# Route logits by 16 fp16 products in four column tiles and one folding product, with the route signs behind both rotations

## The chip, the cores and the metric

The kernel runs on one core of one Trainium2 chip. The metric is the device time of one execution in microseconds (us); the median of three runs stands for a kernel. The profile is of one execution, and its engines are named as it names them: PE is TensorE, PEld its weight loads, DVE is VectorE, ACT is ScalarE, POOL is GpSimd, SP is SyncE. A line number such as L918 is a line of the kernel before.

## The reference, cut to what matters

`x` and `ctx` are (8, 512, 1024) in float32: 4096 tokens of 1024 numbers. The layer adds a recurrent mix of `ctx` to `x` and then a gated attention over the eight batch rows of each time step:

```python
x = x + tanh(g_xattn) * wkv(time_decay, time_first, layernorm(x), ctx)
...
x = silu(x_prev * conv_w[:, 0] + x * conv_w[:, 1])       # h, from layernorm(x)
q = silu(x @ Wq); k = x @ Wk; v = x @ Wv; g = x @ Wg
q = _apply_rotary(q, cos, sin); k = _apply_rotary(k, cos, sin)
logits = jnp.einsum('bhld,hdr->bhlr', v, router_w)        # r = 2 routes, 16 heads
scores = jax.nn.softmax(logits, axis=-1)
onehot = jax.nn.one_hot(jnp.argmax(scores, axis=-1), 2)
sum_ind = jnp.cumsum(onehot, axis=2)
norm = 1.0 / jnp.maximum(sum_ind, 1.0)                    # where sum_ind > 0
q_exp = q * scores * onehot * norm; k_exp = k * onehot    # each route apart
o = (q_exp @ k_exp.T * mask) @ v
out = silu(g) * normalize(o) @ Wout
x = x + tanh(g_ffn) * out
```

With two routes only the difference of the two logits matters: its sign is the route of a head, its size the probability.

## The kernel before, in words

A tile is 16 time steps of all 8 batch rows, 128 tokens, so there are 32 tiles, called steps 0 to 31 here. Every engine runs `pipeline`, which calls its own `step` for each tile. In step i an engine does its part of tile i (`main`), of the recurrence of tile i + 1 (`nxt`), of loads for tile i + 2 (`nxt2`), and of the output of tile i - 1 (`prev`) and i - 2 (`prev2`). Nothing but the order in which `step` is written, and the semaphores, sets the order on an engine; each engine works strictly in that order.

**PE**, step i: route logits (L478, in float32), projection Q in two parts, the gate maximum's small product (L485), projection K, the running sums of the route signs (`sign_sums`, L491), projection V0, transposes of rotated q (L375), projection V1, transposes of rotated k, `same_route` (L497), projection G0, transposes of the gated output, projection G1, `scores` (L520), output projection O0 of the tile before, `xn_transposes` of tile i + 1 (L375, `ps_t<-ident,vx`), `values` (L535), O1, `values` again. A projection is 24 fp16 products of 512 columns: hi by hi (L383), hi by lo (L384) and lo by hi (L387) for eight chunks, so that two fp16 numbers stand for one float32. `same_route` waits for `s_cum`, which `route_coefficients` on DVE sets with its first instruction (L918), because it overwrites the bank that L918 reads. O0 waits for `s_gtlo`, set by L884 on DVE.

**DVE**, step i: the convolution of tile i + 1 from the transposes (`conv_products`, L1003), the low halves `h_lo` (L996), then the head sums (L841), `denominator_terms` (L813, L814, L816), the route signs (`signs`, L906 and L908), the scan (L823) and the sum of the denominator (L833), `rotate` of q (L309, L313 twice, L317), `numerator` (again L813, L814, L816, L823, L833), `route_coefficients` (L918 and four small ones), the gated output, the ratio of the recurrence, and the residual with its statistics.

**ACT**, step i: q through Silu (L634), `route_prob` (L681 and L683, a Tanh of the logits), the copy of k (L638), `seed` (L614, an Exp that needs another table), copies of v, and so on. In step 0 ACT also splits the weights of four more units (`split_unit`, L598, two halves each), the low halves of which DVE makes in `lo_unit` (L775).

**POOL**, step i: the factors of the heads, their product with the gate (L1206), the route signs spread over 512 columns (L1211), `rotate` of k (the same lines L309, L313 twice, L317), and at the end the scales of the norms.

The names: `fa` holds h in float32 while the logits are made, `h_hi` and `h_lo` are its fp16 halves, `w_route` the router folded into the V weights (128 x 8 chunks x 16 heads), `big` is one buffer with many views (the weights, q, k, v, gates, `route`), `small` holds narrow columns, `ps_t`, `ps_g`, `ps_s`, `ps_o` are PSUM banks. Ahead of `pipeline` DVE prepares scales, tables, the folded router (`route_chunk`, L782) and the centred V weights (`centre`, L792, L794, L798).

## Time and profile before

| | us |
|---|---|
| median of three runs | 1753.68 |
| the three runs | 1753.19, 1753.68, 1754.88 |
| the profiled execution, its own time | 1754.45 |
| its span, from the first to the last instruction | 1752.7 |
| PE busy | 1624.3 (93%) |
| DVE busy | 1465.3 (84%) |
| ACT busy | 741.6 (42%) |
| POOL busy | 612.2 (35%) |

The profiled execution took 0.77 us more than the median, and 1.75 us lie around its span. The page's slices show PE busy at 9 tenths from the sixth of 40 slices to the 39th and at the full clock there; in the first five slices DVE is busier than PE.

In a row of the timeline the columns are the start and the length in us, then engine, line, operation, output and input by name, shapes, the count of merged instructions, and in brackets the idle time of the engine before the row with what ended it. Matmuls overlap, so the distance between two starts is what a matmul costs, not its length.

### The profile page before, as it was taken

The numbers are of one execution on the slowest core, as the hardware profiler recorded it, in microseconds if no ns is written. First come the engines' busy times: TensorE is split into PE (matmuls) and PEld (weight loads), VectorE is DVE, ScalarE is ACT, GpSimd is POOL, SyncE is SP. The second block draws the span as 40 slices with busy tenths as digits, with TensorE's granted clock in tenths as the row PEclk, the third lists the DMA queues.
The fourth block names the chain that finished last, engine by engine and source line by source line (L and its number), as shares of the span: only waits on it lengthen the run. The fifth ranks groups of instructions, "written<-read, shape, count | busy, mean of one in ns | idle before, by whom it ended". The sixth has DMA issues, their size and how long they took to land.

```text
span 1752.7 us, 37624 instructions
## 1 busy us (share of the span) xinstructions
PE 1624.3 (93%) x15799; PEld 866.7 (49%) x15799; DVE 1465.3 (84%) x2004; ACT 741.6 (42%) x933; POOL 612.2 (35%) x716
## 2 busy tenths in 40 slices
PE   0445999999999999999999999999999999999996
PEld 0123555555555555555555555555555555555552
DVE  7898988888889888888898888888888888889832
ACT  4835344344443443444434434444344444443420
POOL 1421433443223434432234344322343444223321
PEclk9867999999999999999999999999999999999998
DMA  9500011111100111111111111110001111100000
GB/s 269 191 13 25 5 33 37 37 38 38 28 25 30 29 37 37 37 38 29 27 30 28 37 37 38 37 35 24 30 25 37 38 37 38 37 25 26 14 13 25
DMA packets 23416, 70.77 MB, mean 40 GB/s; under 512 B 2256, under 2 KB 2512, under 8 KB 23248
## 3 DMA queue, kind: packets, MB, share of 16 engines
q1 hardware_dynamic: 23248, 68.37, 13.6%
q8 instruction: 125, 2.05, 0.5%
q14 instruction: 43, 0.35, 0.1%
HBM read 51.59 MB, written 16.78 MB: 39 GB/s over the span
## 4 chain that ended last, share of the span: by engine, by line
PE 88%; DVE 8%; issue 2%; ACT 1%; POOL 1%; DMA 0%; SPq 0%; POOLq 0%; DVEq 0%; ACTq 0%
PE ps_g L383 25%; PE ps_g L384 24%; PE ps_g L387 24%; PE ps_o L535 4%; PE ps_t L478 3%; PE ps_t L375 3%; PE ps_o L375 2%; DVE big L775 2%; PE ps_t L520 1%; PE ps_s L520 1%; DVE seg L823 1%; DVE big L792 0%; PE ps_s L497 0%; DVE seg L814 0%; DMA small<-in_g_ffn 0%
## 5 line engine op out<-in xcount | busy, mean ns | idle before, releaser
L383 PE MATMUL ps_g<-big,h_hi 128*128 128x512 f16 x1536 | 585.5, 381 | 3.2 <-DVE h_lo L996 3.2
L384 PE MATMUL ps_g<-big,h_hi 128*128 128x512 f16 x1536 | 585.4, 381 | 0.0
L387 PE MATMUL ps_g<-big,h_lo 128*128 128x512 f16 x1536 | 584.9, 381 | 0.0
L387 PEld LDWEIGHTS ps_g<-big,h_lo 128*128 128x128 f16 x1536 | 150.7, 98 | 183.8 <-issue 4.2
L1149 POOL TENSOR_TENSOR small<-small 128x1 f32<-128x1 f32 x64 | 14.2, 221 | 648.8 <-DVE small L808 648.6
L383 PEld LDWEIGHTS ps_g<-big,h_hi 128*128 128x128 f16 x1536 | 158.7, 103 | 165.0 <-issue 7.3
L384 PEld LDWEIGHTS ps_g<-big,h_hi 128*128 128x128 f16 x1536 | 150.7, 98 | 165.3 <-issue 3.4
L383 PE MATMUL ps_g<-big 128*128 128x512 f16 x512 | 195.3, 382 | 0.7 <-DVE big L884 0.7
L384 PE MATMUL ps_g<-big 128*128 128x512 f16 x512 | 194.8, 380 | 0.0
L387 PE MATMUL ps_g<-big 128*128 128x512 f16 x512 | 194.7, 380 | 0.0
L1168 POOL TENSOR_TENSOR vx<-vx,ek 128x1024 f32<-128x1024 f32 x32 | 75.3, 2353 | 337.0 <-ACT ek L607 326.1
L823 DVE TENSOR_TENSOR_SCAN seg<-decay,seg 128x1088 f32<-128x1088 f32 x64 | 155.0, 2421 | 1.1
L713 ACT ACTIVATE big<-ps_g,small 128x512 f32<-128x512 f32 x64 | 44.0, 687 | 207.3 <-PE ps_g L387 207.3
L694 ACT ACTIVATE fa<-fa 128x1024 f32<-128x1024 f32 x32 | 33.8, 1058 | 229.7 <-DVE fa L990 229.7
L841 DVE TENSOR_REDUCE small<-big 128x16 f32<-128x1024 f32 x32 | 39.0, 1220 | 71.9 <-ACT big L630 71.9
L1193 POOL TENSOR_TENSOR small<-small 128x16 f32<-128x16 f32 x32 | 93.3, 2914 | 2.5
L804 DVE BATCH_NORM_STATS2 small<-x_ring 128x6 f32<-128x512 f32 x128 | 82.0, 683 | 7.3 <-DMA x_ring<-in_x 6.1
L1206 POOL TENSOR_TENSOR big<-big,small 128x1024 f32<-128x1024 f32 x32 | 86.6, 2706 | 2.5
L1003 DVE TENSOR_TENSOR fa<-ps_t,small 128x512 f32<-128x512 f32 x64 | 43.9, 686 | 49.7 <-PE ps_t L375 49.7
L313 DVE TENSOR_TENSOR big<-big,sin 128x256 f32<-128x256 f32 x64 | 84.2, 1354 | 0.0
L996 DVE SCALAR_TENSOR_TENSOR h_lo<-fa,small,h_hi 128x512 f16<-128x512 f32 x64 | 47.5, 784 | 39.3 <-ACT h_hi L700 39.3
L387 PEld LDWEIGHTS ps_g<-big 128*128 128x128 f16 x512 | 50.2, 98 | 60.9 <-issue 0.8
(158 smaller groups left out, 2902.5 us busy)
## 6 DMA issues: line engine op xcount, KB each, us to landing
x_ring<-in_x SPq DMA_DIRECT2D x32, 512.0 KB
vx<-in_ctx SPq DMA_DIRECT2D x32, 512.0 KB
out<-x_ring SPq DMA_DIRECT2D x32, 512.0 KB
big<-in_wv SPq DMA_DIRECT2D x2, 2048.0 KB, 21.1
big<-in_wg SPq DMA_DIRECT2D x2, 2048.0 KB, 20.7
big<-in_wout SPq DMA_DIRECT2D x2, 2048.0 KB, 20.1
big<-in_wq SPq DMA_DIRECT2D x1, 2048.0 KB, 14.5
big<-in_wk SPq DMA_DIRECT2D x1, 2048.0 KB, 20.1
```

The costliest lines, as they stand in the source:

```text
L313: E.tensor_tensor(t4[:, :, s, :], s4[:, :, 1 - s, :], sin2[:, s * half:(s + 1) * half].rearrange("p (o d) -> p o d", o=1) .to_broadcast([P ...
L375: last = nc.tensor.transpose(order(dst[:, n * P:(n + 1) * P]), src[:, n * P:(n + 1) * P], ident[:, :])
L383: nc.tensor.matmul(dst[:, :], hi, hi_of(u)[:, kc * HALF:(kc + 1) * HALF], start=(kc == 0), stop=False)
L384: nc.tensor.matmul(dst[:, :], hi, lo_of(u)[:, kc * HALF:(kc + 1) * HALF], start=False, stop=False)
L387: last = nc.tensor.matmul(dst[:, :], lo, hi_of(u)[:, kc * HALF:(kc + 1) * HALF], start=False, stop=(kc == KC - 1))
L478: last = nc.tensor.matmul(ps_t[1][:, 0:H], fa[:, kc * P:(kc + 1) * P], w_route[:, kc * H:(kc + 1) * H], start=(kc == 0), stop=(kc == KC - 1))
L535: last = nc.tensor.matmul(ps_o[g][rows, (h - 8 * g) * DV:(h - 8 * g + 1) * DV], probs[rows, h * BLK:(h + 1) * BLK], v[rows, h * DV:(h + 1) ...
L804: last = V.bn_stats(st[:, 6 * g:6 * g + 6], src[:, g * HALF:(g + 1) * HALF])
L823: V.tensor_tensor_scan(seg[:, :], decay[:, :], seg[:, :], 0.0, ALU.mult, ALU.add).then_inc(scanned, 1)
L1168: G.tensor_tensor(vx[:, :], vx[:, :], ek[:, :], ALU.mult).then_inc(s_ev, 1)
L1193: G.tensor_tensor(fac, ftmp, nhalf, ALU.pow).then_inc(s_fp, 1)
L1206: G.tensor_tensor(by_head(sg, DV), by_head(sg, DV), per_head(fac, 0, H, DV), ALU.mult)\
```

## The change

Four edits that belong together:

- **The logits on PE.** The eight float32 products of `fa` with `w_route` go. In their place stand 16 fp16 products, `h_hi` and `h_lo` as moving operands of 128 columns, against `w_route_hl`, 32 columns a chunk (16 of a high half, 16 of a low half). Chunk kc writes 32 rows of the bank, (kc mod 4) x 32 onwards, which are four column tiles of the array. ACT copies the 128 x 128 result to `logits_t` (`copy_logits`), and one float32 product with `r_sum` folds the eight groups of 16 rows and scales them. The 16 products stand behind Q, the folding product behind K.
- **The split of the router's weights.** `split_route_weights` on DVE, ahead of `pipeline`, with a maximum over 1024 columns earlier on.
- **The signs.** On DVE they stand behind the rotation of q instead of ahead of the scan; on PE `sign_sums` stands behind V0 instead of ahead of it; on ACT `route_prob` stands behind the copy of k and in front of `seed` (there it waits for the first instruction of the signs).
- **POOL** rotates k in front of spreading the signs.

```diff
@@ PE, step
                 if main:
-                    if not opening(i):
-                        route_logits(i)
                     unit_ready(i, UQ)
...
                     gate_max_turn(p)
                 if main:
+                    if not opening(i):
+                        route_products(i)
                     unit_ready(i, UK)
                     bank_free(i, 1, prev2)
                     project(ps_g[1], h_hi, h_lo, UK, s_kp)
                     if opening(i):
                         for r in range(5, 9):
                             bound_row(r)
-                        pe.wait_ge(s_wroute, 8)
-                        route_logits(i)
-                    sign_sums(i)
+                        pe.wait_ge(s_rw, 8)
+                        route_products(i)
+                    route_logits(i)
                     unit_ready(i, UV)
                     after(pe, s_q, i + 1)
                     project(ps_g[0], h_hi, h_lo, UV, s_vp)
+                    sign_sums(i)
@@ PE
+            def route_products(i):
+
+                after(pe, s_hlo, 2 * (i + 1))
+                for a in (h_hi, h_lo):
+                    for kc in range(KC):
+                        rows = slice(kc % 4 * 2 * H, (kc % 4 + 1) * 2 * H)
+                        last = nc.tensor.matmul(ps_t[1][rows, 0:P], w_route_hl[:, kc * 2 * H:(kc + 1) * 2 * H],
+                                                a[:, kc * P:(kc + 1) * P], start=(a is h_hi and kc < 4),
+                                                stop=(a is h_lo and kc >= 4))
+                last.then_inc(s_dlp, 1)
+
             def route_logits(i):
 
-                after(pe, s_h, i + 1)
-                for kc in range(KC):
-                    last = nc.tensor.matmul(ps_t[1][:, 0:H], fa[:, kc * P:(kc + 1) * P], w_route[:, kc * H:(kc + 1) * H],
-                                            start=(kc == 0), stop=(kc == KC - 1))
-                last.then_inc(s_dl, 1)
+                after(pe, s_dlc, i + 1)
+                nc.tensor.matmul(ps_t[1][:, P:P + H], logits_t, r_sum, start=True, stop=True).then_inc(s_dl, 1)
@@ ACT, step
                     if not opening(i):
-                        route_prob(i)
+                        copy_logits(i)
                     act.wait_ge(s_kp, i + 1)
                     A(k_sb, ps_g[1][:, :], ACT.Copy, scale=inv[:, UK:UK + 1]).then_inc(s_k, 1)
                     if opening(i):
-                        route_prob(i)
+                        copy_logits(i)
+                    route_prob(i)
                 if nxt:
                     seed(n)
@@ ACT
+            def copy_logits(i):
+                act.wait_ge(s_dlp, i + 1)
+                after(act, s_dl, i)
+                A(logits_t, ps_t[1][:, 0:P], ACT.Copy).then_inc(s_dlc, 1)
@@ DVE, ahead of the pipeline
+            def split_route_weights():
+
+                V.tensor_reduce(r_sum, ident[:, :].rearrange("p (j h) -> p h j", h=H), AX_X, ALU.add).then_inc(s_rw, 1)
...
+                V.tensor_scalar(r_bound, r_max, mx[:, UV:UV + 1], mx[:, UV + 1:UV + 2], ALU.mult, ALU.max).then_inc(s_rw, 1)
...
+                V.tensor_scalar(r_bound, r_bound, TINY, None, ALU.max).then_inc(s_rw, 1)
...
+                V.reciprocal(r_scale, r_bound).then_inc(s_rw, 1)
...
+                V.tensor_scalar(r_scale, r_scale, W_TOP, None, ALU.mult).then_inc(s_rw, 1)
+                V.tensor_scalar(r_inv, r_bound, mx[:, U:U + 1], LN_BOUND / (W_TOP * H_TOP), ALU.mult, ALU.mult)\
+                 .then_inc(s_rw, 1)
...
+                V.tensor_scalar(r_sum, r_sum, r_inv, None, ALU.mult).then_inc(s_rws, 1)
+                V.tensor_scalar(hl[:, :, 0, :], rows, r_scale, None, ALU.mult).then_inc(s_rws, 1)
+                dve.wait_ge(s_rws, 2)
+                V.scalar_tensor_tensor(hl[:, :, 1, :], rows, r_scale, hl[:, :, 0, :], ALU.mult, ALU.subtract)\
+                 .then_inc(s_rw, 1)
...
             tokens_by_time()
+            dve.wait_ge(s_base, 1)
+            V.tensor_reduce(r_max, x_ring[:, 2, :], AX_X, ALU.max, apply_absolute_value=True).then_inc(s_rw, 1)
...
                 route_chunk(m)
+            split_route_weights()
             centre(UV + 1)
@@ DVE, step
                     denominator_terms(n)
-                if main:
-                    signs(i)
-                if nxt:
                     denominator_scan(n)
...
                     rotate(dve, V, i, 0, q_sb, rot_q, s_r1q, s_rq)
+                    signs(i)
                     if opening(i):
                         lo_unit(4)
@@ POOL, step
                 if main:
+                    pool.wait_ge(s_k, i + 1)
+                    after(pool, s_op, 2 * i)
+                    rotate(pool, G, i, 1, k_sb, rot_k, s_r1k, s_rk)
                     pool.wait_ge(s_sgn, i + 1)
                     after(pool, s_rt, i)
                     G.tensor_tensor(by_head(route, BLK), per_head(sgn, 0, H, BLK),
                                     fold.rearrange("p (o l) -> p o l", o=1).to_broadcast([P, H, BLK]), ALU.mult)\
                      .then_inc(s_route, 1)
-                    pool.wait_ge(s_k, i + 1)
-                    after(pool, s_op, 2 * i)
-                    rotate(pool, G, i, 1, k_sb, rot_k, s_r1k, s_rk)
```

What stands in a row on DVE in the middle of a step, from the last denominator term to the first instruction of the numerator, first before and then after the change (L906 and L908 are the signs, L948 and L950 in the changed kernel):

```order
L816 TENSOR_TENSOR fa<-seg,small 128x1024
L906 TENSOR_SCALAR small<-ps_t 128x16
L908 TENSOR_SCALAR small<-small 128x16
L823 SCALAR_TENSOR_TENSOR seg<-decay,seg 128x1088
L825 COPY carry_b<-seg 128x64
L833 TENSOR_TENSOR fa<-fa,seg 128x1024
L913 TENSOR_TENSOR small<-small,ps_s 128x2
L309 TENSOR_TENSOR big<-big,cos 128x512
L313 TENSOR_TENSOR big<-big,sin 128x16x16 x2
L317 TENSOR_TENSOR big<-big 128x512
L813 COPY seg<-carry_a 128x64
```

```order
L860 TENSOR_TENSOR fa<-seg,small 128x1024
L867 SCALAR_TENSOR_TENSOR seg<-decay,seg 128x1088
L869 COPY carry_b<-seg 128x64
L877 TENSOR_TENSOR fa<-fa,seg 128x1024
L955 TENSOR_TENSOR small<-small,ps_s 128x2
L314 TENSOR_TENSOR big<-big,cos 128x512
L318 TENSOR_TENSOR big<-big,sin 128x16x16 x2
L322 TENSOR_TENSOR big<-big 128x512
L948 TENSOR_SCALAR small<-ps_t 128x16
L950 TENSOR_SCALAR small<-small 128x16
L857 COPY seg<-carry_a 128x64
```

The same eleven instructions stand there; the two signs moved from the second place to the last but one, behind the four of the rotation.

On POOL, from the gate's product on (L1206, L1250 after), before and after; L1211 and L1258 spread the signs:

```order
L1206 TENSOR_TENSOR big<-big,small 128x1024
L1211 TENSOR_TENSOR big<-small,big 128x512
L309 TENSOR_TENSOR big<-big,cos 128x512
L313 TENSOR_TENSOR big<-big,sin 128x16x16 x2
L317 TENSOR_TENSOR big<-big 128x512
```

```order
L1250 TENSOR_TENSOR big<-big,small 128x1024
L314 TENSOR_TENSOR big<-big,cos 128x512
L318 TENSOR_TENSOR big<-big,sin 128x16x16 x2
L322 TENSOR_TENSOR big<-big 128x512
L1258 TENSOR_TENSOR big<-small,big 128x512
```

The spreading of the signs moved from in front of the four instructions of the rotation to behind them.

On ACT in step 0, from the Silu of q to the next weights' high halves (L598 before, L612 after), before and after:

```order
L634 ACTIVATE big<-ps_g,small 128x512
L638 ACTIVATE big<-ps_g,small 128x512
L681 ACTIVATE small<-ps_t 128x16
L683 ACTIVATE small<-small 128x16
L614 ACT_TABLE_LOAD
L614 ACTIVATE ek<-fa,small 128x1024
L598 ACTIVATE big<-big,small 128x2048 x2
```

```order
L648 ACTIVATE big<-ps_g,small 128x512
L652 ACTIVATE big<-ps_g,small 128x512
L696 ACTIVATE big<-ps_t 128x128
L701 ACTIVATE small<-ps_t 128x16
L703 ACTIVATE small<-small 128x16
L628 ACT_TABLE_LOAD
L628 ACTIVATE ek<-fa,small 128x1024
L612 ACTIVATE big<-big,small 128x2048 x2
```

Here ACT keeps its order but for the added copy (L696); what moved is the sign on DVE that L701 waits for.

## Rows read from the trace of the kernel before

**Rows 1.** Busy us of PE, PEld, DVE, ACT, POOL, then clock, DMA share, GB/s, 214:1664

```profile
214.00:1664.00 1450.00, 1449.99 (x14308) 774.63 (x14306) 1251.86 (x1712) 618.74 (x812) 533.93 (x636) 1.00 0.12 33
```

**Rows 2.** Timeline of PE in one middle step: logits, sign sums, same_route, next transposes

```profile
872.96 1.96 PE L478 MATMUL ps_t<-big,fa 128*128 128x16 f32 x16
874.77 0.38 PE L383 MATMUL ps_g<-big,h_hi 128*128 128x512 f16 x1
...
885.26 0.29 PE L491 MATMUL ps_s<-small,causal_m 128*128 128x16 f32 x2
885.40 0.38 PE L383 MATMUL ps_g<-big,h_hi 128*128 128x512 f16 x1
...
896.63 0.38 PE L497 MATMUL ps_s<-big 128*128 128x512 bf16 x1
```

**Rows 3.** Timeline of DVE in the same step, from the convolution to route_coefficients

```profile
865.39 0.69 DVE L1003 TENSOR_TENSOR fa<-ps_t,small 128x512 f32<-128x512 f32 x1 [1.62 <-PE ps_t L375]
...
875.36 1.22 DVE L841 TENSOR_REDUCE small<-big 128x16 f32<-128x1024 f32 x1 [2.33 <-ACT big L630]
...
878.03 1.23 DVE L816 TENSOR_TENSOR fa<-seg,small 128x1024 f32<-128x1024 f32 x1
879.18 0.17 DVE L906 TENSOR_SCALAR small<-ps_t 128x16 f32<-128x16 f32 x1
...
879.46 2.42 DVE L823 TENSOR_TENSOR_SCAN seg<-decay,seg 128x1088 f32<-128x1088 f32 x1
...
883.28 2.32 DVE L309 TENSOR_TENSOR big<-big,cos 128x512 f32<-128x512 f32 x1
885.52 2.67 DVE L313 TENSOR_TENSOR big<-big,sin 128x256 f32<-128x256 f32 x2
888.23 1.10 DVE L317 TENSOR_TENSOR big<-big 128x512 f32<-128x512 f32 x1
889.26 0.74 DVE L813 COPY seg<-carry_a 128x64 f32<-128x64 f32 x1
...
896.14 0.17 DVE L918 TENSOR_TENSOR small<-ps_s,small 128x16 f32<-128x16 f32 x1
```

**Rows 4.** Timeline of step 1: its convolution, same_route on PE, the next convolution

```profile
166.34 0.69 DVE L1003 TENSOR_TENSOR fa<-ps_t,small 128x512 f32<-128x512 f32 x1
...
197.39 0.38 PE L497 MATMUL ps_s<-big 128*128 128x512 bf16 x1 [0.72 <-DVE small L918]
...
216.11 0.69 DVE L1003 TENSOR_TENSOR fa<-ps_t,small 128x512 f32<-128x512 f32 x1 [1.47 <-PE ps_t L375]
```

**Rows 5.** Timeline of POOL and ACT in the middle step, beside the rotation of q

```profile
885.01 1.50 POOL L1211 TENSOR_TENSOR big<-small,big 128x512 bf16<-128x512 f32 x1
885.47 0.69 ACT L638 ACTIVATE big<-ps_g,small 128x512 f32<-128x512 f32 x1 [4.31 <-PE ps_g L387]
...
886.47 1.44 POOL L309 TENSOR_TENSOR big<-big,cos 128x512 f32<-128x512 f32 x1
...
890.00 1.28 POOL L317 TENSOR_TENSOR big<-big 128x512 f32<-128x512 f32 x1
```

**Rows 6.** Timeline of the setup: one short DVE instruction beside POOL, and without it

```profile
75.99 2.37 POOL L1176 TENSOR_TENSOR big<-big,x_ring 128x1024 f32<-128x1024 f32 x1
...
77.73 0.69 DVE L794 TENSOR_SCALAR big<-big 128x64 f32<-128x64 f32 x1
...
94.35 0.20 DVE L794 TENSOR_SCALAR big<-big 128x64 f32<-128x64 f32 x1
```

**Rows 7.** Timeline of step 0: ACT's table, seed and weight halves; DVE's low half

```profile
117.42 1.28 ACT L614 ACT_TABLE_LOAD   x1
...
122.66 1.15 ACT L614 ACTIVATE ek<-fa,small 128x1024 f32<-128x1024 int32 x1 [3.95 <-DVE fa L833]
123.71 3.88 ACT L598 ACTIVATE big<-big,small 128x2048 f16<-128x2048 f32 x2
...
126.68 4.80 DVE L775 SCALAR_TENSOR_TENSOR big<-big,small 128x2048 f16<-128x2048 f32 x2
```

More of the change, by code:

```diff
@@ L127, in flamingo_layer @@
         w_route = turn[:, P:2 * P]
+        w_route_hl = turn[:, 2 * P:3 * P].bitcast(F16)
+        logits_t = turn[:, 3 * P:4 * P]
         q_sb = work[:, 4 * C:4 * C + HALF]
@@ L148, in flamingo_layer @@
         cnt_c = sb("cnt_c", [P, 1])
-        small = sb("small", [P, 373])
+        small = sb("small", [P, 378])
         at = [0]
@@ L185, in flamingo_layer @@
         usc = col(2)
+        r_max, r_bound, r_scale, r_inv = col(1), col(1), col(1), col(1)
+        r_sum = col(H)
         seed_b, minus_one, half_c = col(1), col(1), col(1)
@@ L680, in route_prob @@
                 after(act, s_cf, i)
-                A(pr, ps_t[1][:, 0:H], ACT.Abs).then_inc(s_th, 1)
+                A(pr, ps_t[1][:, P:P + H], ACT.Abs).then_inc(s_th, 1)
                 act.wait_ge(s_th, 2 * i + 1)
@@ L784, in route_chunk @@
                  .then_inc(s_wroute, 1)
+            def split_route_weights():
+                V.tensor_reduce(r_sum, ident[:, :].rearrange("p (j h) -> p h j", h=H), AX_X, ALU.add).then_inc(s_rw, 1)
+                dve.wait_ge(s_rw, 2)
+                dve.wait_ge(s_wsc, UV + 2)
+                V.tensor_scalar(r_bound, r_max, mx[:, UV:UV + 1], mx[:, UV + 1:UV + 2], ALU.mult, ALU.max).then_inc(s_rw, 1)
+                dve.wait_ge(s_rw, 3)
+                V.tensor_scalar(r_bound, r_bound, TINY, None, ALU.max).then_inc(s_rw, 1)
+                dve.wait_ge(s_rw, 4)
+                V.reciprocal(r_scale, r_bound).then_inc(s_rw, 1)
+                dve.wait_ge(s_rw, 5)
+                V.tensor_scalar(r_scale, r_scale, W_TOP, None, ALU.mult).then_inc(s_rw, 1)
+                V.tensor_scalar(r_inv, r_bound, mx[:, U:U + 1], LN_BOUND / (W_TOP * H_TOP), ALU.mult, ALU.mult)\
+                 .then_inc(s_rw, 1)
+                dve.wait_ge(s_rw, 7)
+                dve.wait_ge(s_wroute, 8)
+                hl = w_route_hl.rearrange("p (k s h) -> p k s h", s=2, h=H)
+                rows = w_route.rearrange("p (k h) -> p k h", h=H)
+                V.tensor_scalar(r_sum, r_sum, r_inv, None, ALU.mult).then_inc(s_rws, 1)
[3 more added lines that the diff above has]
+                 .then_inc(s_rw, 1)
             def centre(u):
@@ L905, in signs @@
                 after(dve, s_cump, i)
-                V.tensor_scalar(sgn, ps_t[1][:, 0:H], 0.0, 2.0, ALU.is_ge, ALU.mult).then_inc(s_sgp, 1)
+                V.tensor_scalar(sgn, ps_t[1][:, P:P + H], 0.0, 2.0, ALU.is_ge, ALU.mult).then_inc(s_sgp, 1)
                 dve.wait_ge(s_sgp, i + 1)
@@ L940, in denominator_terms @@
                 after(dve, s_pre, n)
-                after(dve, s_dl, n)
                 recurrence_terms(n, ek[:, :], carry_b, s_sva, s_ekt, fa[:, :], s_fda)
```

3 lines of the change are left out of this document (2 added, 1 removed).

## The prediction

> **What bounds the kernel now.** I read the busy time by stretch first. From 214 to 1664 us PE is busy all 1450 us at the full clock, and DVE 1251.86 us of it [rows 1]. So PE is the bound of the steady part, and a microsecond less on PE in each step seems to be worth 31 us. The timeline of one step tells how far that holds. A cycle is the time from one convolution to the next: 216.11 to 865.39 is 13 cycles, 49.94 us each [rows 3, 4]. DVE's idle times in it are 1.62 us before the convolution, where it waits for PE's transposes, and 2.33 us before the head sums, where it waits for ACT [rows 3]. From there to L918 one instruction follows the other. And PE waits for L918 before same_route: L918 ends at 896.31, same_route starts at 896.63 [rows 2, 3]. Step 1 shows how much of these 0.32 us is slack. There PE was early, idle for 0.72 us until L918, and same_route started 0.31 us after L918's start, against 0.49 us in the middle step. Slack is 0.18 us. The cycle of step 1 took 49.77 us [rows 4]. That is the floor which the loop through DVE sets, whatever PE does: transposes of the next tile, convolution, ACT, DVE's chain to L918, same_route, and PE's work from same_route to the next transposes, which the change leaves alone. PE's work that does get shorter lies beside DVE's chain.
>
> **PE, part by part.** Removed: the eight float32 products, 872.96 to 874.77, 1.81 us a step [rows 2]. Added: the folding product. A float32 product of 16 columns costs 885.26 to 885.40, 0.14 us [rows 2]. Added: 16 fp16 products of 128 columns in four column tiles. No row has that form. Upper bound: a product record of L478 costs 1.81 / 16 = 0.113 us with its weight load behind nothing, so 16 cost 1.81 us. Lower bound: a projection's product of 512 columns goes on every 0.216 us, so 128 columns are 0.054 us, and four rounds of four tiles at once are 0.22 us. I take 0.5 us, near the lower end, since the work of a full round is at most a quarter of a projection's and two changes of the array's form have to be paid; it lies in PE's cover anyway. PE's own cycle would then be 49.94 - 1.81 + 0.14 + 0.5 = 48.77 us, 1.0 us under the floor of 49.77. Nearly all of the gain turns into a wait, and the question is what the change does to the floor.
>
> **DVE's chain.** The signs leave their place ahead of the scan. L816 ends at 879.26 and the scan started at 879.46; it can start some 0.04 us after L816, so 0.16 us are gained there [rows 3]. Next is the rotation. Its four instructions are long because DVE and POOL take turns: L309 takes 2.32 us, the second and third 2.67 us together, L317 1.10 us, while POOL runs without a gap [rows 3, 5]. Before, three POOL instructions take their turn between the end of L309 and the end of L317: L1211, L309 and the first L313. After, POOL has the rotation of k first, so they are L309 and both L313. For that k must be there by the end of DVE's L309 at 885.44. k's copy ended at 885.47 + 0.69 = 886.16 [rows 5]; K's end moves forward by the logits and back by the 16 products, 1.81 - 0.5 = 1.31 us, so k is there at 884.85. The turn of L1211 lasted from DVE's end of L309 at 885.60 to 886.51, 0.91 us; the turn of the second L313 lasted from the end of L317 at 889.33 to 890.00 less 0.08 of the copy, 0.59 us. The exchange gains 0.32 us, and L317 ends at 889.33 - 0.16 - 0.32 = 888.85. POOL's L317 follows, which takes 1.14 to 1.28 us [rows 5], to 890.0 to 890.13.
>
> Now the signs stand here. The first reads PSUM and can run beside it. The second goes from SBUF to SBUF like L794, which took 0.69 us beside a POOL instruction and 0.20 us without one [rows 6]. So I let it wait for POOL's L317. It ends at about 890.15, the copy L813 (0.22 us free of POOL, starting 0.09 before that end) at 890.25 instead of 890.00. The chain to L918 is 0.25 us longer and the floor 50.02 us.
>
> The Trainium skill (SBUF — State Buffer, Who interferes with whom) says that a tensor_scalar or copy from SBUF to SBUF can take a form that uses both ports, and that it then waits until GpSimd's instruction has ended. The trace agrees, 0.69 against 0.20 us; by that rule the second sign waits too.
>
> Projection V0 began at 885.40 and takes 24 x 0.216 = 5.18 us; now it ends 1.31 us earlier, at 889.3. There PE meets the sign sums, and the sign is ready at 890.15, a wait of about 0.9 us; V1 and the transposes then end by 896.6, as L918's result allows same_route at 896.7. The spreading of the signs on POOL starts at 890.2 and needs 0.91 us; the next DVE instruction with two inputs in SBUF starts at 891.4, so it doesn't meet it. ACT waits for the first sign until 889.0 and then has Tanh, table and seed done by 892; the ratio needs them at 898. That wait costs nothing in a steady step.
>
> Thirty cycles lie between the convolution of step 1 and that of tile 31 (166.34 to 1664.4, 1498.0 us: one of 49.77 and 29 of 49.94). After: 30 x 50.02 = 1500.6, **+2.6 us**. The last step has no recurrence on DVE, PE sets it, and it gains 1.81 - 0.64 = **-1.2 us**.
>
> **Setup and step 0.** Until about 196 us the chain of work that ended last runs through DVE, so DVE's additions count in full. One maximum over 1024 columns, 1.2 us (as L841 [rows 3]); one reduction, 0.3; six short instructions of 0.20 (as L794 alone [rows 6]), 1.2; two of 128 columns, 0.3 each: **+3.3 us**, with no idle time of DVE behind them that they fill. In step 0 the second weight split waits on ACT. ACT's table load stood at 117.42 and was done long before the seed at 122.66; the weight halves ran from 123.71 and DVE's L775 took them without a wait at 126.68 [rows 7]. After, signs come behind the rotation. POOL rotates k earlier there, which by the turns above ends DVE's rotation some 1.7 us earlier, so the sign is at ACT by 125.2 on the same scale; then 0.45 for Abs and Tanh, 1.28 table, 1.15 seed, 1.95 for the first half: L775 can start at 130.05 instead of 126.68, **+3.4 us** (+5 if the rotation ends no earlier, 0 if DVE's later waits in this step would have come anyway; none stands in its timeline).
>
> **The sum.** 3.3 + 3.4 + 2.6 - 1.2 = +8.1 us on the profiled execution's 1754.45, 1762.6 us; less its 0.77 us over the median, 1761.8.
>
> **Rivals.**
> (a) The second sign does not wait for POOL (for it: it has 16 columns, L794 had 64; against: rows 6). The copy L813 waits for it instead, the chain is 0.07 us longer, the floor 49.84: 30 x 49.84 - 1498.0 = -2.8. Sum 3.3 + 3.4 - 2.8 - 1.2 = +2.7, 1756.4 us. Within 0.2%, not slower.
> (b) DVE's chain opens up: if k came after DVE has done its four instructions, they would not share turns with POOL, the chain would be over 2 us shorter and PE's own 48.77 us would hold: 30 x 48.77 - 1498.0 = -34.9, sum -29.4, 1724 us, faster. It decides at a k ready after 887, against 884.85 by my sum; partly late values lie between.
> (c) The column tiles don't run side by side, so the change doesn't do on PE what it says: 16 products cost 1.81 + 0.1 us. PE's cycle is 50.18, over the floor. 30 x 50.18 - 1498.0 = +7.4; last step +0.2; sum 14.3, 1768 us. It decides from 1.7 us on. The Trainium skill (TensorE: Matmul & The Clock Gate, Part 3, The mechanism) says that a weight load overlaps a matmul in flight only when the row group differs; column tiles share all rows, so that rule speaks for (c). The rows show only that loads do hide in the full-array form.
> (d) POOL's spreading of the signs catches the next two-input instruction on DVE and pushes it by 0.9 us: floor 50.8, +25 us more, 1784 us. The margin is 0.2 us.
>
> **Chances.** Forecast 0.48, (a) 0.27, (b) 0.08, (c) 0.10, (d) 0.07. The range 1755 to 1769 takes in (a), the forecast with +3.4 to +5 in step 0, and (c). Measurement of this kernel tells 0.2%, 3.5 us, from no change. Slower by more: nearly all of the forecast, a fifth of (a), (c) and (d), 0.69. Same: 0.23. Faster: 0.08.
>
> **What the profile after would show.** In a middle step PE idle for about 1.0 us in all, before the sign sums (released by the second sign) and before same_route (by the changed L918), DVE's distance from convolution to L918's start 31.0 us against 30.75, cycles of 50.0 us; the 16 products within 0.3 to 0.7 us; in step 0 DVE idle for 4 to 5 us before its low half, released by ACT. Wrong would be: PE busy without a gap and cycles under 49.5 us (b), or over 50.1 with no gap (c).

## The result, and the profile after

The changed kernel takes 1758.33 us (median of 12 runs, 1757.57 to 1759.41) against 1754.53 us for the kernel before on the same chips: ratio 1.0023, with a 95% interval of 1.0014 to 1.0032. It is slower by 3.8 us. The profiled spans are 1756.2 and 1752.7 us.

Busy time first: the page's line of busy time and share of the span, then the stretch of [rows 1], with the same columns.

```profile
PE 1598.1 (91%) x15863; PEld 821.9 (47%) x15863; DVE 1468.7 (84%) x2014; ACT 746.7 (43%) x965; POOL 602.2 (34%) x716
```

```profile
214.00:1664.00 1450.00, 1428.26 (x14486) 735.20 (x14483) 1256.76 (x1716) 624.03 (x842) 527.76 (x640) 1.00 0.12 33
```

PE was busy all 1450 us before [rows 1]; now it is idle for 21.7 of them, and nothing is won: in the steady part the cycle, the distance from one convolution to the next, has a median of 49.91 us against 49.93. PE's waits from 215 to 1670 us say where the idle time is (engine, tile and line waited for; total us, times, longest):

```profile
PE ps_s L505 <- DVE small L950: 20.6, 29, 1.0
```

L505 are the sign sums and L950 is the second sign. PE's timeline of a middle step (start, us, line, form; in brackets the idle time and who ended it), as [rows 2]:

```profile
883.55 0.28 PE L499 MATMUL ps_s<-small,big 128*128 128x1 f32 x2
883.76 0.30 PE L486 MATMUL ps_t<-h_hi,big 128*32 128x128 f16 x8
883.88 0.29 PE L486 MATMUL ps_t<-h_lo,big 128*32 128x128 f16 x8
884.10 0.39 PE L388 MATMUL ps_g<-big,h_hi 128*128 128x512 f16 x1
...
895.45 0.40 PE L505 MATMUL ps_s<-small,causal_m 128*128 128x16 f32 x2 [0.68 <-DVE small L950]
...
901.97 0.38 PE L511 MATMUL ps_s<-big 128*128 128x512 bf16 x1
```

The 16 products (L486) take 0.34 us, from 883.76 to 884.10, where the eight float32 ones took 1.81. DVE in the same step, as [rows 3]:

```profile
870.79 0.69 DVE L1044 TENSOR_TENSOR fa<-ps_t,small 128x512 f32<-128x512 f32 x1 [1.48 <-PE ps_t L380]
...
880.76 1.22 DVE L885 TENSOR_REDUCE small<-big 128x16 f32<-128x1024 f32 x1 [2.33 <-ACT big L644]
...
888.51 2.32 DVE L314 TENSOR_TENSOR big<-big,cos 128x512 f32<-128x512 f32 x1
890.75 2.36 DVE L318 TENSOR_TENSOR big<-big,sin 128x256 f32<-128x256 f32 x2
893.14 1.10 DVE L322 TENSOR_TENSOR big<-big 128x512 f32<-128x512 f32 x1
894.16 0.16 DVE L948 TENSOR_SCALAR small<-ps_t 128x16 f32<-128x16 f32 x1
894.36 1.03 DVE L950 TENSOR_SCALAR small<-small 128x16 f32<-128x16 f32 x1
895.31 0.21 DVE L857 COPY seg<-carry_a 128x64 f32<-128x64 f32 x1
...
896.67 1.22 DVE L860 TENSOR_TENSOR fb<-seg,small 128x1024 f32<-128x1024 f32 x1
...
901.65 0.17 DVE L960 TENSOR_TENSOR small<-ps_s,small 128x16 f32<-128x16 f32 x1
...
920.70 0.69 DVE L1044 TENSOR_TENSOR fa<-ps_t,small 128x512 f32<-128x512 f32 x1 [1.47 <-PE ps_t L380]
```

And ACT's copy of k and POOL beside it, as [rows 5]:

```profile
889.49 0.69 ACT L652 ACTIVATE big<-ps_g,small 128x512 f32<-128x512 f32 x1 [4.89 <-PE ps_g L392]
890.25 1.70 POOL L314 TENSOR_TENSOR big<-big,cos 128x512 f32<-128x512 f32 x1
891.92 1.78 POOL L318 TENSOR_TENSOR big<-big,sin 128x256 f32<-128x256 f32 x2
893.77 1.59 POOL L322 TENSOR_TENSOR big<-big 128x512 f32<-128x512 f32 x1
895.47 1.05 POOL L1258 TENSOR_TENSOR big<-small,big 128x512 bf16<-128x512 f32 x1
```

The second sign (L950) has 16 columns and takes 1.03 us: it ends at 895.39, right behind POOL's L322 (895.36). The carry copy behind it is ready at 24.73 us after the convolution, 24.61 before. From the convolution to the start of route_coefficients (L960) it is 30.86 us, against 30.75 before [rows 3].

Step 0 is the other place. ACT's wait for the first sign, and DVE's wait for ACT's weight half, which was not there in [rows 7]:

```profile
127.34 0.18 ACT L701 ACTIVATE small<-ps_t 128x16 f32<-128x16 f32 x1 [10.77 <-DVE small L948]
...
130.13 3.88 ACT L612 ACTIVATE big<-big,small 128x2048 f16<-128x2048 f32 x2
132.15 2.35 DVE L795 SCALAR_TENSOR_TENSOR big<-big,small 128x2048 f16<-128x2048 f32 x1 [4.64 <-ACT big L612]
```

| stretch | before, us | after, us | difference | forecast |
|---|---|---|---|---|
| to the last low half of the setup (L775, L795) | 109.54 | 112.05 | +2.51 | +3.3 |
| to the convolution in step 1 | 166.34 | 171.81 | +5.47 in all, so step 0 +2.96 | +6.7, step 0 +3.4 |
| 30 cycles, to the convolution of tile 31 | 1498.09 | 1498.24 | +0.15 | +2.6 |
| last step, to its same_route | 31.24 | 30.04 | -1.20 | -1.2 |
| from there to the end of DVE's last instruction | 50.68 | 49.78 | -0.90 | 0 |

The last output's DMA follows, 6.3 us in both. Together the differences are +3.5 us, that of the profiled spans.

### The profile page after: what moved, and what is told of

Its sections match the earlier page's. It is cut to its first block, busy times and chain, and to the rows that moved or that the text cites. A ratio compares the mean times of both kernels' runs of the same rounds, so it can differ in the third digit from the quotient of the medians.

```text
span 1756.2 us, 37826 instructions
## 1 busy us (share of the span) xinstructions
PE 1598.1 (91%) x15863; PEld 821.9 (47%) x15863; DVE 1468.7 (84%) x2014; ACT 746.7 (43%) x965; POOL 602.2 (34%) x716
## 3 DMA queue, kind: packets, MB, share of 16 engines
q8 instruction: 125, 2.05, 0.5%
## 4 chain that ended last, share of the span: by engine, by line
PE 46%; DVE 35%; ACT 10%; issue 8%; POOL 1%; DMA 0%; DVEq 0%; SPq 0%; ACTq 0%; POOLq 0%
PE ps_g L388 13%; PE ps_g L392 12%; PE ps_g L389 12%; DVE seg L867 5%; DVE big L318 4%; DVE big L314 4%; DVE fa L860 2%; PE ps_t L380 2%; DVE seg L858 2%; DVE seg L1047 2%; ACT L621 2%; DVE fa L877 2%; DVE fa L1031 2%; ACT fa L714 2%; ACT ek L621 2%
## 5 line engine op out<-in xcount | busy, mean ns | idle before, releaser
L388 PEld LDWEIGHTS ps_g<-big,h_hi 128*128 128x128 f16 x1536 | 153.5, 100 | 174.1 <-issue 11.2
L389 PEld LDWEIGHTS ps_g<-big,h_hi 128*128 128x128 f16 x1536 | 150.9, 98 | 165.3 <-issue 3.6
L733 ACT ACTIVATE big<-ps_g,small 128x512 f32<-128x512 f32 x64 | 43.4, 678 | 106.0 <-PE ps_g L392 106.0
L1250 POOL TENSOR_TENSOR big<-big,small 128x1024 f32<-128x1024 f32 x32 | 86.7, 2708 | 2.5
L652 ACT ACTIVATE big<-ps_g,small 128x512 f32<-128x512 f32 x32 | 22.0, 687 | 151.4 <-PE ps_g L392 151.4
L634 ACT ACTIVATE ek<-fa,small 128x1024 f32<-128x1024 f32 x32 | 36.8, 1149 | 106.7 <-DVE fb L1002 106.7
```

The source lines that it names most:

```text
L388: nc.tensor.matmul(dst[:, :], hi, hi_of(u)[:, kc * HALF:(kc + 1) * HALF], start=(kc == 0), stop=False)
L389: nc.tensor.matmul(dst[:, :], hi, lo_of(u)[:, kc * HALF:(kc + 1) * HALF], start=False, stop=False)
L1250: G.tensor_tensor(by_head(sg, DV), by_head(sg, DV), per_head(fac, 0, H, DV), ALU.mult)\
```

## The experiments

In the order in which they ran. A cycle is the median of the distances between convolutions. Differences from "the changed kernel" are from its 1758.33 us; ratios are to the kernel before, run beside the variant.

**DVE's denominator ahead of the head sums**, in the changed kernel and in the one before (there with `signs` left behind it):

```diff
+                if nxt:
+                    denominator_terms(n)
                 if prev:
                     dve.wait_ge(s_sq, 2 * (p + 1))
                     V.tensor_reduce(ossq, ...)
                 if nxt:
-                    denominator_terms(n)
                     denominator_scan(n)
```

> The changed kernel with DVE's copy, transpose and product of the denominator (for the next tile) put ahead of the head sums, into the place where DVE waits 2.33 us for ACT's squares. Theory (the loop through DVE sets the cycle, PE has room): DVE waits only until ACT's second exponential has ended at 879.76 and the scan starts at about 883.55 instead of 884.68, so the cycle falls from 49.91 by up to 1.1 us to 48.8, still over PE's own 48.6: 30 x 1.1 = 33 us less, 1725 us. Rival 1 (PE's own time sets the cycle, the 16 products cost what they replace): 1758 us, no change, and PE without a gap. Rival 2 (the head sums come 1.5 us later, POOL's head factors, gate product and rotation of k follow, and PE waits for the rotated k): the cycle falls by 0.3 to 0.6 us only, 1740 to 1750 us, with PE's wait at the transposes of k.

> The same exchange on DVE, made in the kernel before (float32 logits on PE, signs ahead of the scan). Theory (two limits within 0.2 us of each other, PE's own 49.9 and DVE's loop 49.77): only DVE's loop gets shorter, PE's own 49.9 us stays, so the cycle moves by at most 0.05 us: 1752 to 1755 us, no change. Rival (PE was never a limit, only DVE's loop): the cycle falls by as much as in the changed kernel, 15 to 33 us in all, 1721 to 1740 us.

Measured: 1873.2 us (ratio 1.068) and 1907.49 us (1.087), cycles of 54.2 and 55.0 us. Neither expectation held. DVE's gap was filled, and the loss came through POOL, far beyond what rival 2 had put on it. The timeline of DVE and POOL in the changed kernel's variant, and PE's waits (215 to 1660 us):

```profile
885.14 2.41 DVE L867 TENSOR_TENSOR_SCAN seg<-decay,seg 128x1088 f32<-128x1088 f32 x1
885.30 2.26 POOL L1230 TENSOR_TENSOR small<-small 128x16 f32<-128x16 f32 x1 [2.29 <-DVE small L887]
...
896.51 1.93 POOL L1251 TENSOR_TENSOR big<-big,small 128x1024 f32<-128x1024 f32 x1
```

```profile
PE ps_t L380 <- POOL big L322: 59.0, 27, 2.5
PE ps_s L511 <- POOL big L1259: 33.3, 27, 1.3
```

A head factor of 16 columns (L1230) takes 2.26 us beside the scan, against 0.22 where it stood beside DVE's transpose. One by one they meet the scan and the products; the gate product starts 24.92 us after the convolution (896.51 - 871.59) instead of 16.73, and POOL's rotation and the signs' spreading behind it make PE wait. So the 2.33 us gap of DVE isn't free: work put into it delays the head sums, and POOL gets its operands from them. For the two limits this pair settles nothing, since a third one, POOL, was made the bound in both.

**Step 0: the weight half first.**

```diff
-                    route_prob(i)
+                    else:
+                        route_prob(i)
 ...
                     if opening(i):
                         split_unit(4)
+                        route_prob(i)
```

> The changed kernel with one edit in step 0 alone: ACT takes the seed and the high half of the fifth weight unit first, and the Abs and Tanh of the route logits behind them, so that the weight half no longer waits for the first sign, which now stands behind DVE's rotation. Theory (the late sign costs 2.96 us through ACT in step 0): 2.0 to 3.0 us less than the changed kernel, about 1755.5 us; DVE's wait for ACT in front of the low half falls from 4.64 to under 2 us. Rival (another wait of step 0, for PE or for the next low half, comes as late anyway): within 0.5 us of the changed kernel, 1758 us.

Measured: 1754.74 us (1753.48 to 1756.68), 3.6 under the changed kernel and more than the 2 to 3 expected; cycles as in it, 49.91; the convolution in step 1 at 168.37 instead of 171.81. DVE's wait fell from 4.64 to 0.82 us. That takes back 3.44 us where step 0 had lost 2.96, so ACT's wait for the sign was the whole of step 0's term.

**The 16 products four times.**

```diff
-                for a in (h_hi, h_lo):
+                for a in (h_hi, h_lo, h_hi, h_lo, h_hi, h_lo, h_hi, h_lo):
```

> The changed kernel with the 16 products of a step issued four times over (64 products; the result is the same, since each round of sums starts anew). It prices the products and PE's room in the cycle. Theory (16 products cost 0.25 to 0.35 us, since four column tiles run side by side, and PE has 1.0 us of room a cycle, most of it in front of the sign sums): 48 more products are 0.75 to 1.05 us, they fill the room, and the cycle grows by 0 to 0.1 us: 1758 to 1762 us. Rival (column tiles run one after the other, 0.05 to 0.1 us a product): 48 more cost 2.6 to 5.4 us, 1.6 to 4.4 of them over the room: 1806 to 1890 us.

Measured: 1753.79 us, 4.5 us *less* than the changed kernel, cycle 49.73. Neither had that. The price of the products was right: a step's eight L486 groups follow each other at 0.11 us, 0.0143 us a product.

```profile
882.31 0.30 PE L486 MATMUL ps_t<-h_hi,big 128*32 128x128 f16 x8
...
883.11 0.29 PE L486 MATMUL ps_t<-h_lo,big 128*32 128x128 f16 x8
883.32 0.39 PE L388 MATMUL ps_g<-big,h_hi 128*128 128x512 f16 x1
```

PE's work grew by 0.67 us and its waits at the sign sums fell from 20.6 to 0.8 us. The gain is on DVE (this kernel's convolution is at 869.35):

```profile
888.72 0.69 ACT L652 ACTIVATE big<-ps_g,small 128x512 f32<-128x512 f32 x1 [5.00 <-PE ps_g L392]
889.29 1.82 DVE L318 TENSOR_TENSOR big<-big,sin 128x256 f32<-128x256 f32 x2
889.48 1.35 POOL L314 TENSOR_TENSOR big<-big,cos 128x512 f32<-128x512 f32 x1 [0.66 <-ACT big L652]
...
892.37 0.50 DVE L950 TENSOR_SCALAR small<-small 128x16 f32<-128x16 f32 x1
...
894.15 2.12 DVE L860 TENSOR_TENSOR fb<-seg,small 128x1024 f32<-128x1024 f32 x1
```

k is there at 889.41, 20.06 us after the convolution, instead of 19.39. DVE's first rotation instruction ends at 20.02, so its second is already running when POOL begins, and the two L318 take 1.82 instead of 2.36 us. The numerator's product (L860) then meets POOL and takes 2.12 instead of 1.22 us, which gives most of it back; 0.18 us a cycle stay.

**No rotation of k on POOL**, in both kernels (it is left out; k goes to PE as it is):

```diff
-                    rotate(pool, G, i, 1, k_sb, rot_k, s_r1k, s_rk)
...
-                    transposes(ps_t[1], rot_k, s_ktp, as_is)
+                    transposes(ps_t[1], k_sb, s_ktp, as_is)
```

> The changed kernel without POOL's rotation of k (its four instructions are left out, PE transposes k as ACT wrote it, so the scores are not the reference's). Theory (the cycle of the changed kernel is set by DVE's chain, and that by the turns which DVE and POOL take, while PE has about 1.0 us of room): DVE's rotation behind its first instruction is no longer shared, DVE's loop falls by over 2 us to about 47.2, and PE's own time shows, 49.91 - 1.0 = 48.9 us a cycle: 1728 us (1722 to 1735). Rival (PE has no such room, its saving is not there): under 0.3 us a cycle, 1750 us or more.

> The same left out of the kernel before (the scores are not the reference's). Theory (PE's own time is at the limit there, with the float32 logits in it): the cycle stays within 0.1 us of 49.93, 1751 to 1755 us, though DVE's loop falls by about 2 us. Rival (only DVE's loop sets the cycle in both kernels): it falls as in the changed kernel without the rotation, to 1722 to 1735 us.

Measured: 1721.65 us (ratio 0.981) and 1751.42 us (0.998). Cycles 48.73 and 49.93. The view of busy time, 300 to 1600 us, of the changed kernel, of it without the rotation, and of the kernel before without it:

```profile
300.00:1600.00 1300.00, 1280.40 (x12878) 658.69 (x12876) 1126.71 (x1537) 558.85 (x754) 472.80 (x572) 1.00 0.12 33
```

```profile
300.00:1600.00 1300.00, 1298.64 (x13260) 678.53 (x13285) 1081.04 (x1571) 571.97 (x774) 350.80 (x482) 1.00 0.12 34
```

```profile
300.00:1600.00 1300.00, 1298.63 (x12807) 695.17 (x12831) 1074.32 (x1536) 553.58 (x731) 357.39 (x468) 1.00 0.12 33
```

With DVE's chain shortened (the coefficients start at 28.08 us after the convolution in the changed kernel without the rotation) PE is busy throughout in both, and the cycle is PE's own: 49.93 us before the change, 48.73 after. The change does save 1.20 us of PE a step, and in the real kernel all of it is hidden behind DVE's chain. The same removal is worth 36.7 us after the change and 3.7 us before it, and of these 3.7 nothing is in the cycle.

**POOL's old order** in the changed kernel (spreading the signs ahead of the rotation of k):

> The changed kernel with POOL's order of before: the spreading of the signs first, the rotation of k behind it. Since the signs now stand behind DVE's rotation, POOL starts the rotation of k only when DVE's is done. Theory (the exchange on POOL is needed once the signs are moved): DVE's rotation is over about 2 us sooner, but POOL rotates k from about 893.7 on, in turns with the numerator's products and behind its scan, and is done about 900, where PE wants k at 896.6: cycle 52 to 53.5 us, 1820 to 1870 us, PE waiting at the transposes of k for POOL. Rival (POOL keeps up, the order on POOL is of no account): 1755 to 1761 us.

Measured: 1764.56 us (ratio 1.0053), cycle 50.18. The direction is the theory's, the size is a tenth of it. DVE's rotation did end 2.0 us sooner (21.43 us after the convolution, 23.45 in the changed kernel), and POOL's work met the numerator (POOL's timeline, convolution at 873.23, and PE's waits):

```profile
897.27 4.51 POOL L318 TENSOR_TENSOR big<-big,sin 128x256 f32<-128x256 f32 x2
901.87 2.25 POOL L322 TENSOR_TENSOR big<-big 128x512 f32<-128x512 f32 x1
```

```profile
PE ps_t L380 <- POOL big L322: 34.9, 28, 1.6
```

POOL is done at 904.12, 30.89 us after the convolution. PE's transposes of k start at 904.26 after a wait of 1.25 us, so PE wanted it at 29.78. The size in the expectation was a slip: its 900 us was on the clock of the trace after (29.2 us after the convolution there) and its 896.6 on that of the trace before (31.2 us after it). Set against one convolution, POOL was to be done before PE wants it, and the wait comes from its being done 1.7 us later than estimated.

**POOL's rotation waits for DVE's first rotation instruction.**

```diff
                     after(pool, s_op, 2 * i)
+                    pool.wait_ge(s_r1q, 3 * i + 1)
                     rotate(pool, G, i, 1, k_sb, rot_k, s_r1k, s_rk)
```

> The changed kernel with one wait more: POOL's rotation of k also waits for DVE's first rotation instruction of the same step. In the run with 64 products k came 0.7 us later, just behind that instruction, and the cycle was 49.73 us; here k is as early as in the changed kernel and PE has no work more. Theory (the late k itself gave that: DVE's second instruction gets in ahead of POOL's first, and DVE is done 0.5 us sooner): cycle 49.7 to 49.8, 1752 to 1755 us, and PE idle again for about 0.8 us before the sign sums. Rival (the work on PE gave it, by no waits of PE at the sign sums): cycle 49.91, 1758 us.

Measured: 1751.32 us (1750.54 to 1753.03), ratio 0.9979 with an interval of 0.9969 to 0.9988; cycle 49.73. It is the late start of POOL's rotation, not PE's extra work, that gave the gain: k is as early as in the changed kernel (19.39) and PE again waits, about 1.0 us a step. It does so for route_coefficients (L960), not in front of the sign sums as expected. One added wait beats both kernels.

Nine of the 30 cycles are shorter, mostly 49.57 us. In both kinds POOL's spreading of the signs (L1258) and DVE's product (L860) start within 0.01 us of each other, 24.82 us after the convolution. In 21 cycles POOL is first: L860 takes about 2.12 us and the scan behind it 2.42. In nine DVE is: 1.22 and 3.15, and the coefficients start at 30.54 instead of 30.71.

**The signs in one instruction.**

```diff
-                V.tensor_scalar(sgn, ps_t[1][:, P:P + H], 0.0, 2.0, ALU.is_ge, ALU.mult)
-                V.tensor_scalar(sgn, sgn, -1.0, None, ALU.add)
+                V.tensor_scalar(sgn, ps_t[1][:, P:P + H], 0.0, 0.5, ALU.is_ge, ALU.subtract)
```

> The changed kernel with the signs taken in one instruction that reads PSUM and gives +0.5 and -0.5 (the count of signs is then multiplied by 4, exactly), so there is no second sign that goes from SBUF to SBUF. Theory (what costs is the turn of POOL's last rotation instruction, which any copy or sign from SBUF to SBUF waits for): the carry copy behind it waits for the same POOL instruction, so DVE's chain is shorter by 0 to 0.1 us; cycle 49.8 to 49.92, 1755 to 1758.5 us; PE's wait at the sign sums falls to about 0.2 us, and PE waits later. Rival (the second instruction and its wait are themselves the cost, as the forecast had it with 0.25 us and more): cycle 49.65 or less, under 1751 us.

Measured: 1757.21 us, cycle 49.84. As the theory had it: the carry copy now waits for the same POOL instruction, 1.20 us long, and the second sign costs 0.07 us a cycle. PE's wait in front of the sign sums is gone, and PE waits in front of same_route instead, for the first of the route coefficients (L958 here; same_route's own record is missing in this trace, so the wait is shown at the product behind it). The waits from 215 to 1640 us:

```profile
PE ps_g L388 <- DVE small L958: 31.8, 28, 1.2
```

So the sign sums were where PE waited, and not what set the cycle.

```profile
893.55 1.60 POOL L322 TENSOR_TENSOR big<-big 128x512 f32<-128x512 f32 x1
893.94 0.16 DVE L948 TENSOR_SCALAR small<-ps_t 128x16 f32<-128x16 f32 x1
894.03 1.20 DVE L857 COPY seg<-carry_a 128x64 f32<-128x64 f32 x1
```

**All 16 products in one column tile.**

```diff
-                        rows = slice(kc % 4 * 2 * H, (kc % 4 + 1) * 2 * H)
+                        rows = slice(0, 2 * H)
```

> The changed kernel with all 16 products in one column tile of 32 rows (one sum over the eight chunks and both halves, the folding product over 32 rows; the result is the same up to rounding). Theory (the four tiles run side by side, 0.0143 us a product in the run of 64): one tile costs a projection's rate, 128 of 512 columns of 0.216 us, 0.054 us a product, 16 in 0.87 us, 0.6 more than with four tiles; k then comes 0.6 us later, just about with the end of DVE's first rotation instruction, and the cycle is between 49.73 and 49.91: 1753 to 1758 us. Rival (the tiles don't matter, consecutive products overlap anyhow): 16 in 0.25 to 0.35 us and 1758 us.

Measured: 1755.52 us, cycle 49.74.

```profile
883.04 0.62 PE L486 MATMUL ps_t<-h_hi,big 128*32 128x128 f16 x8
883.50 0.61 PE L486 MATMUL ps_t<-h_lo,big 128*32 128x128 f16 x8
884.04 0.39 PE L388 MATMUL ps_g<-big,h_hi 128*128 128x512 f16 x1
```

The products take 1.00 us instead of 0.34, a little over the 0.87 expected: eight of them 0.46 us in one tile, where eight in the row of 64 over four tiles took 0.11. The four column tiles do run side by side. k comes at 20.05, with the end of DVE's first instruction, so the kernel with the dearer products is 2.8 us faster than the changed one.

**Both repairs together**, then the wait for the third rotation instruction (`3 * i + 3`) in place of the first.

> The changed kernel with two of the edits above together: in step 0 ACT takes the weight half ahead of Abs and Tanh, and POOL's rotation of k waits for DVE's first rotation instruction. Theory (the two act in different places, step 0 and the cycle, and add up): 7.0 + 3.6 us under the changed kernel's 1758.3, 1747.7 us (1746.5 to 1749). Rival (they overlap, or the wait on POOL was already what helped in step 0): 1750 to 1751.5 us.

> As the run before, but POOL's rotation of k waits for DVE's third rotation instruction. Theory (every POOL instruction that gets its turn inside DVE's rotation costs DVE a turn): DVE's second and third take 0.4 us each, its last still meets POOL's first, and the rotation ends about 0.4 us sooner than with the wait for the first; POOL's last rotation instruction ends no sooner and pushes the numerator's product as before, so of the 0.4 us between none and all reaches the cycle: 49.35 to 49.75, 1736 to 1749 us. Rival (the k rotation comes too late for PE or pushes the numerator's product further): cycle over 49.8, 1751 us or more, with PE waiting for the rotated k or for the route coefficients.

Measured: 1748.21 us (0.9964, 0.9949 to 0.9978) and 1742.22 us (0.9927, 0.9912 to 0.9942). The two add up, 10.1 us against 3.6 + 7.0. The wait for the third gives a cycle of 49.51. Its step (convolution at 861.27):

```profile
881.23 0.75 DVE L318 TENSOR_TENSOR big<-big,sin 128x256 f32<-128x256 f32 x2
882.01 0.69 DVE L322 TENSOR_TENSOR big<-big 128x512 f32<-128x512 f32 x1
882.14 1.69 POOL L314 TENSOR_TENSOR big<-big,cos 128x512 f32<-128x512 f32 x1 [1.39 <-DVE big L318]
...
885.15 1.22 DVE L862 TENSOR_TENSOR fb<-seg,small 128x1024 f32<-128x1024 f32 x1
885.32 2.17 POOL L322 TENSOR_TENSOR big<-big 128x512 f32<-128x512 f32 x1
886.40 3.37 DVE L869 TENSOR_TENSOR_SCAN seg<-decay,seg 128x1088 f32<-128x1088 f32 x1
```

DVE's rotation meets no POOL instruction any more and ends 21.43 us after the convolution instead of 23.45. The expectation had its last instruction meet POOL's first; it did not. POOL's turns come later, one of them ahead of the scan (3.37 instead of 2.42 us), and route_coefficients start at 30.47 instead of 30.86. It is the fastest version here that still computes the layer, 16.1 us under the changed kernel.

| kernel | k there | DVE's rotation ends | carry copy ends | coefficients start | cycle |
|---|---|---|---|---|---|
| before | 20.77 | 23.94 | 24.61 | 30.75 | 49.93 (PE) |
| after | 19.39 | 23.45 | 24.73 | 30.86 | 49.91 |
| products x4 | 20.06 | 22.90 | 23.64 | 30.68 | 49.73 |
| one tile | 20.05 | 22.91 | 23.66 | 30.70 | 49.74 |
| k after the first | 19.39 | 22.92 | 23.67 | 30.71 | 49.73 |
| k after the third | 19.39 | 21.43 | 22.72 | 30.47 | 49.51 |
| one sign | 19.39 | 23.45 | 24.67 | 30.81 | 49.84 |
| POOL's old order | 19.39 | 21.43 | 21.95 | 29.69 | 50.18 (POOL) |
| after, k not rotated | 19.39 | 21.42 | 21.95 | 28.08 | 48.73 (PE) |

Times in us after the convolution of a middle step. The last column is the median cycle.

The table shows which wait sets the cycle. In the six kernels where it names neither PE nor POOL, the cycle is 19.02 to 19.05 us longer than the start of the coefficients, whatever PE does before it; in step 1 before it is 19.03 (197.39 - 0.31 - 166.34 = 30.74, of 49.77). Where PE or POOL is the bound it is 19.18 or more.

## Why the prediction was right, and where its sizes were off

The forecast was slower, because PE's saving turns into a wait while setup and step 0 get longer. That is what happened, and the runs without k's rotation show it: PE's own cycle is 48.73 us, worked out as 48.77. The sum was +8.1 us, and it is +3.8 (+3.5 in the profiled spans). That is in the range, but nearer to the +2.7 of rival (a) than to the forecast, though (a)'s mechanism was not at work, and only just outside the 3.5 us that the prediction counted as no change. The steady part, to which most of the working went, gave next to nothing; slower came from setup and step 0, +5.47 us together. That the direction stood with a floor priced at twice its size is in part luck. Four terms carry the difference: the floor 2.4 us of it, setup 0.8, step 0 0.4 and the stretch behind the last step 0.9.

- **The floor.** This is the term that was mis-sized most: +0.25 us was worked out, and +0.11 (30.86 - 30.75) to +0.14 (49.91 - 49.77 in step 1 before) came. That is a cycle of 49.91 instead of 50.02, and 30 cycles gave +0.15 instead of +2.6 us. The steps of the working held: DVE's rotation ended at 23.45 us after the convolution against 23.46 worked out, and the second sign did wait for POOL's last rotation instruction, as the rule of the Trainium skill (SBUF — State Buffer, Who interferes with whom) also had it; the trace agrees, 1.03 us against 0.17 where POOL is idle in step 0. But POOL's instruction ended at 24.57, not between 24.61 and 24.74, so the sign ended at 24.60 instead of 24.76 and the carry copy at 24.73 instead of 24.86. A tenth of a microsecond on a floor counts thirty times, 3.3 us here; three cycles of 50.2 to 50.3 us gave 0.9 back. The rows could not give it closer.
- **Setup.** +2.51 instead of +3.3. The maximum (1.13 us) and the split (90.28 to 92.41, 2.13 us) cost 3.26, as worked out. Of it 0.25 has nothing to do with the change: DVE was that much earlier before its first added instruction (the scan that starts at 18.51 in the trace before starts at 18.27 in this one). And 0.49 was made up at one later short instruction, the one of [rows 6]: it took 0.69 us beside POOL before, and takes 0.20 now, since POOL's turn is over when it comes. "No idle time of DVE behind them that they fill" overlooked that a turn of POOL is idle time of DVE too.
- **Step 0.** +2.96 instead of +3.4, through the mechanism named. DVE's rotation ended 2.05 us earlier, not 1.7 (at 127.22 less the setup's 2.51, against 126.76), and with it the sign. The run with the weight half first takes back 3.44 us there.
- **PE and the last step.** The 16 products cost 0.34 us, and the change of form around them about 0.13 more: PE's cycle fell by 1.20 us (49.93 - 48.73), which is 1.81 - 0.14 less 0.47. The prediction had put 0.5 on both together. The last step gains 1.20 us as forecast.
- **Behind the last step.** 0.9 us less, where nothing was forecast, and not by the change. Up to the last output projection the two traces agree (37.51 and 37.52 us from same_route). Of that projection the first nine products go on at about 0.43 us in the profile before and the first five in the one after, the others at 0.22: PE's granted clock was at half (1.2 of 2.4 GHz) for 13.7 us there before and for 10.2 us after. It fell while PE was idle (1721.4 to 1730.6 us in the profile before). In the first four variants the whole stretch took 49.45 to 50.01 us. What sets the moment at which the clock comes back is not shown.

**The rivals.** (a) did not come about, and the run with one sign shows what it would have been: 49.84 us a cycle, the very floor that it had. (c) is out: 0.0143 us a product in four tiles, 1.00 against 0.34 us when one tile takes them all. The rule of the Trainium skill (TensorE: Matmul & The Clock Gate, Part 3, The mechanism), by which weight loads overlap a product in flight only with another row group, does not hold for these column tiles: products one behind the other have different weights and use the same rows. The measurement decides. (b) and (d) were nearer than 0.08 and 0.07 say, and not apart from each other. The point from which (b) acts is k at 20.04 us after the convolution, the end of DVE's first rotation instruction, and the changed kernel has it at 19.39; 0.65 us more and DVE's rotation gets shorter. What (b) left out is that POOL's turns don't go away, they move on to the numerator's product, which is (d)'s mechanism. In the changed kernel (d) stayed out by 0.15 us: POOL's spreading of the signs (L1258) ended at 896.52 and DVE's product (L860) started at 896.67. In the kernels whose rotation ends at 22.9 it came, and L860 takes 2.12 us in the steps shown. So the prize was 0.2 us a cycle with k a little later, 0.4 with POOL held back further, and in no run with the rotation PE's 48.73.

**The signs named beforehand.** DVE idle for 4.64 us before the low half (4 to 5 forecast), the products at 0.34 us (0.3 to 0.7) and cycles of 49.91 (50.0) came. PE was idle for 0.7 us a cycle and not 1.0, all of it before the sign sums and none before same_route.

## What to carry to other kernels

Time taken from the busiest engine can be worth nothing, as here, where the second loop stood 0.16 us a cycle behind it. Measure that loop first: look for the one step in which the busy engine waited, for there its floor stands. Where two engines take turns, as DVE and POOL do here, the order of their turns sets that floor: shifting an operand's arrival by 0.7 us, or holding the other engine back by a wait, was worth more here than 1.2 us of TensorE work. An idle gap on one engine may be what feeds another: fill it only after asking who waits for the work that it delays.

## What the runs showed of the hardware

- Four column tiles of 128 x 32 take fp16 products of 128 columns side by side: in a row of 64 each costs 0.0143 us, in one tile 0.46 / 8 = 0.058. A short row gains less, 16 products take 0.34 us against 1.00.
- DVE instructions with two inputs in SBUF, and signs and copies from SBUF to SBUF, were not at work together with POOL's, down to 16 columns. A sign of 16 columns took 1.03 us beside POOL's rotation and 0.17 without; POOL's product of 16 columns took 2.26 us beside a scan on DVE. A sign read from PSUM took 0.16 us beside POOL (L948), and DVE's transpose and POOL did not hold each other up: L858 took 1.23 us with and without POOL beside it, and POOL's product of 16 columns 0.22 us beside it.
- While both were waiting, the turns went to and fro by single instructions. In the changed kernel's middle step the ends are, from the end of DVE's first rotation instruction on: DVE 890.83, POOL 891.95, DVE 892.23, POOL 892.83, DVE 893.10, POOL 893.69, DVE 894.24, POOL 895.36, DVE 895.39. It is not so when one begins to wait only at the moment the other ends: with the products four times, DVE's L860 started at 894.15, 0.04 us before POOL's L322 ended, and POOL's next one still came first.
- So the cost of sharing depends on which of the two is waiting when an instruction ends: DVE's four rotation instructions took 5.73 us (17.72 to 23.45) with k there 0.65 us before the first of them ended, 5.20 us with k 0.04 us behind that end, and 3.71 us with POOL held back.
- At half the granted clock a projection's product of 512 columns went on every 0.43 us, at the full clock every 0.216.
- In every kernel but the pair with the early denominator a few cycles in the middle are 0.2 to 0.6 us longer, often at about the same tiles. What makes them so was not tried.
